# Group 6's maxima one unit later and in another bank, and sixteen idle matmuls in the first four attention units

## The chip, the cores and the metric

The kernel runs on one core of one Trainium2 chip. The metric is the device time of one execution in microseconds (us), and the number compared is the median of several runs. Before the change the median of three runs is 684.25 us (682.8 to 686.36).

## The reference, cut to what matters

The kernel computes one transformer layer on x of shape (4, 1024, 256): cross attention with a context of 64 rows per batch, and a feed-forward part with one shared expert and eight routed ones (two per token). Only the attention is touched by the change:

```
q = (layernorm(x) @ Wq + bq)   in 16 heads of width 16
k = (ctx @ Wk + bk),  v = (ctx @ Wv + bv)      64 keys per batch
a = clip(q k^T / 4, -10000, 10000)
a = softmax(a);  a = 1/64 everywhere if anything in it is not a number
x = x + (a v) @ Wo + bo
x = x + shared(layernorm(x)) + sum over the top 2 experts of w * expert(layernorm(x))
```

The softmax subtracts, for every query row and head, the maximum over the keys. The kernel computes these maxima in a separate, cheaper pass.

## The kernel before, in words

The 4096 rows of x are 32 tiles of 128, in NG = 8 groups of four tiles (n = 0 to 7) and in NU = 16 attention units of two tiles (u = 0 to 15). Every engine has its own instruction stream, written out by hand, and semaphores join them; within an engine the order is that of the code. Most products are made in three half-precision parts (high times high, high times low, low times high).

Before the attention units, TensorE projects the queries of each group and makes the *row scores* `row_scores(js)`: for each tile and each half of the heads one 128x512 matmul, whose maximum over the keys VectorE takes in `row_max` (L1094). There are 64 of them (j = 0 to 63). A group's eight maxima are clipped (`clip_max` on VectorE L1103, or for the last two groups `clip_late` on GpSimd L700), transposed by TensorE in `max_t(n)` (L1581, four transposes) into bank `max_bank(n)`, and copied by VectorE to `m_t` in `copy_max(n)` (L1109). Groups 0 to 4 go before the units, group 5 at the end of unit 0, group 6 at the end of unit 2, group 7 at the end of unit 12. The last row scores are made inside units 0, 1 (four each) and 4 to 11 (one each, in bank 7).

TensorE's `unit(u)` for the attention is: `scores(u)`, 24 matmuls of 32 rows x 256 into banks 0 to 3, which waits until all four exponentials of unit u-1 have been taken; the late row scores; then for r = 0 to 3 `weigh(u-2, r)`, 12 matmuls of 34 or 32 columns with the probabilities of two units back, which waits for GpSimd's low half (`pl_ready`), and `subtract_max(u, r)`, two matmuls of 32 rows x 256, which waits for VectorE's `clip` (L1129) of bank r; the rest of the late row scores; `max_t`; and from unit 4 on `project(u-4)`, one matmul with 512 columns and twelve with 256 into bank 6, which waits for the output's transposes by DMA (`ot_got`, issued on SP at L540 after GpSimd's L722).

ScalarE per unit: four exponentials `exps(u, r)` (L900), three casts to half precision `cast_p` (L907), the high half of the output (L952) and the fourth cast; in units 1 to 3 also a weight cast (L893). GpSimd per unit: in units 0 to 2 two multiplications for the low half of the keys (`keys`, L652), four low halves of the probabilities (L729), the low half of the output (L722), `clip_late(6)` first in unit 2, and the weight split `low_weight(1)` (L707) in unit 3. VectorE per unit: four clips, `copy_max` if there is one, late maxima, residual and statistics of unit u-5 (L1169 on), `normalise(u-2)` (L1141, L1149), and in units 3 and 5 a weight split `split_lo` (L1189). In unit 0 VectorE also makes the scale of the exponentials from a flag that lies in bank 7 (`scale_of_exps`, L1122 to L1124, which raises `scale_ready`), between its first and its second clip.

Bank 7 holds that flag, group 6's and 7's transposed maxima and the row scores from j = 56 on; bank 6 holds the transposed maxima of groups 0 to 5 and from unit 4 on the projection.

Of the kernel before, what the change touches and what calls it, by code (L numbers as in the profile page):

```python
# [12 lines left out]
P = 128  # L13
# [4 lines left out]
def build(nc, x, ctx_t, wq, bq, wk, bk, wv, bv, wo, bo, gate_t, w_all, out):  # L18
# [14 lines left out]
    NG = NT // GT  # L33
# [34 lines left out]
    with ExitStack() as ctx:  # L68
# [6 lines left out]
        bank = [ctx.enter_context(nc.psum_tensor(f"bank{i}", [P, 512], F32)) for i in range(8)]  # L75
# [290 lines left out]

        def max_bank(n):

            return 6 if n < NG - 2 else 7

        def score_bank(j):

# [672 lines left out]
        def _(dve):  # L1045
# [145 lines left out]
            def unit(u):  # L1191
                if u == NU - 1:
                    scale_guess2(slice(0, LN2_FIRST * GT))
                    scale_and_shift2(slice(0, LN2_FIRST * GT))
                for r in range(RT):
                    clip(u, r)
                    if u == 0 and r == 0:
                        scale_of_exps()
                if u == 0:
                    copy_max(NG - 4)  # L1200
                if u == 1:
                    copy_max(NG - 3)
                if u == 3:
                    copy_max(NG - 2)
                if u == 13:
                    copy_max(NG - 1)
                if u < 2:
                    late_max(u)
                if known(u, 5):
                    rows_of(u - 5)  # L1210
                if known(u, 2):
                    normalise(u - 2)
                if u >= 2:
                    late_max(u)
                if u == 3:
                    split_lo(0)
                if u == 5:
                    split_lo(2)
                if NU <= u < NU + 3:
                    low_half(u - NU)  # L1220
# [311 lines left out]
        def _(pe):  # L1532
            def mm(o, a, b, first, last, check=False):
                return pe.matmul(o, a, b, start=first, stop=last, skip_group_check=not check)  # L1534
# [19 lines left out]
            def row_scores(js):  # L1554

                for j in js:
                    t, hf = divmod(j, HF)
                    n, i = divmod(t, GT)
                    if i == 0 and hf == 0:
                        pe.wait_ge(kblk_ready, HF * (n * B // NG + 1))  # L1560
                    pe.wait_ge(qh_ready, HF * n + hf + 1)
                    if t > 0:
                        pe.wait_ge(smax_used, scores_read_for(j))
                    if j == LATE_MAX:
                        pe.wait_ge(mt_copied, NG - 1)
                    mm(bank[score_bank(j)][:, :], qx[:, 0, hf, bass.ts(t, P)],
                       k_blk[:, 0, n * B // NG, hf].rearrange("p h k -> p (h k)"),
                       True, True).then_inc(smax_ready, 1)

            def max_t(n):  # L1570
                if n < NG - 2:
                    pe.wait_ge(mcl_ready, n + 1)
                else:
                    pe.wait_ge(mcl_late, n - NG + 3)
                if n == NG - 2:
                    pe.wait_ge(scale_ready, 1)
                elif 1 <= n < NG - 2:
                    pe.wait_ge(mt_copied, n)
                for i in range(GT):
                    c = 64 * i  # L1580
                    ins = pe.transpose(bank[max_bank(n)][:, c:c + 64].bitcast(F16),  # L1581
                                       m_cl[:, n % 2, i].rearrange("p r h -> p (r h)"), ident[:, :])
                ins.then_inc(mt_ready, 1)
# [116 lines left out]
            def project(u):  # L1700

                pe.wait_ge(ot_got[u % 2], 16 * UT * (u // 2 + 1))
                if u == 0:
                    pe.wait_ge(bo_split, UT)
                    pe.wait_ge(wo_lo, 1)
                    pe.wait_ge(mt_copied, NG - 2)
                if u >= 1:
                    pe.wait_ge(y_added, u)
                mm(bank[6][:, :], ones_h[0:P // 2, :], bo_hl.rearrange("p t c -> p (t c)"), True, False)
                for t in range(UT):  # L1710
                    for i, (a, c) in enumerate(THREE):
                        for hf in range(HF):
                            ins = mm(bank[6][:, bass.ts(t, C)], o_t[:, u % 2, t, c, hf],
                                     wo_hl[:, a, hf], False, i == 2 and hf == HF - 1)
                ins.then_inc(y_ready, 1)
# [8 lines left out]
            def gate(g):  # L1724
# [13 lines left out]
                                     c == 1 and hf == HF - 1)  # L1738
                ins.then_inc(lg_ready, 1)

            def unit(u):
                if known(u, 0):
                    scores(u)
                row_scores(late_scores(u)[:2])
                for r in range(RT):
                    if known(u, 2):
                        weigh(u - 2, r)
                    if known(u, 0):
                        subtract_max(u, r)
                if u < 2:  # L1750
                    row_scores(late_scores(u)[2:])
                if u == 0:
                    max_t(NG - 3)
                if u == 2:
                    max_t(NG - 2)
                if u == 12:
                    max_t(NG - 1)
# [205 lines left out]
```

## Time and profile before

| | |
|---|---|
| median of three runs | 684.25 us |
| the profiled execution's own time | 689.7 us |
| its span, first to last instruction | 688.0 us |
| mean granted clock of TensorE | 0.935 |
| busy: TensorE matmul | 606.8 us (88%) |
| busy: VectorE, ScalarE, GpSimd | 413.8, 346.7, 395.3 us |

The span runs from the first to the last instruction; 1.7 us of the execution's own time lie outside it. The granted clock is given as a share of full speed: 1.00 is 2.4 GHz and 0.50 is 1.2 GHz. The page cuts the span into 40 slices of 17.2 us; the attention units are the slices 5 to 11 (from about 78 to 205 us). In those slices the page's clock row reads 9, 5, 5, 9, 9, 7, 7. A matmul's busy time is counted as long as it is in the pipeline, so an engine that reads as fully busy need not be at its peak.

### The profile page before, as it was taken

Reading aid. Unit: us, or ns where it says so; the run is one execution under the profiler, and the core shown is the slowest. Engines: PE = TensorE matmul, PEld = TensorE weight load, DVE = VectorE, ACT = ScalarE, POOL = GpSimd, SP = SyncE. Lnnn points to the kernel's source line nnn. Section 1 sums busy time; section 2 is a strip of 40 time slices with the busy share of each in tenths; the row PEclk is TensorE's granted clock in tenths of the full one; section 3 lists DMA queues with packets and bytes.
Section 4 is the critical chain, followed back from the end, with each engine's and each line's share of the span. In section 5 each row is a group of like instructions: output and inputs, shape, how many; then the busy total and the mean of one; then the engine's idle time right before and its main releaser. Section 6 shows DMA issues by size and latency. Waiting matters only on the chain.

```text
span 688.0 us, 15439 instructions
## 1 busy us (share of the span) xinstructions
PE 606.8 (88%) x5212; PEld 412.9 (60%) x5212; DVE 413.8 (60%) x916; ACT 346.7 (50%) x572; POOL 395.3 (57%) x333
## 2 busy tenths in 40 slices
PE   3698679999897897997998999999999999999990
PEld 1244235665564554554754788777788787776870
DVE  5998866986875453899654344544444545443450
ACT  3987577886697662653254343333332433333330
POOL 6589598989660121434063546666656666657543
PEclk9899855997789998999999999999999999999996
DMA  8344401251129796885149544766755657657533
GB/s 266 90 70 84 131 2 40 51 129 33 32 61 216 172 206 204 214 161 116 46 102 175 103 78 88 109 91 100 101 95 96 97 96 101 93 95 101 87 40 39
DMA packets 121102, 72.44 MB, mean 105 GB/s; under 512 B 91779, under 2 KB 114246, under 8 KB 121030
## 3 DMA queue, kind: packets, MB, share of 16 engines
q1 hardware_dynamic: 101974, 44.01, 29.2%
q0 software_dynamic: 19056, 27.43, 24.8%
q8 instruction: 49, 0.80, 0.5%
q14 instruction: 23, 0.19, 0.1%
HBM read 29.47 MB, written 22.15 MB: 75 GB/s over the span
## 4 chain that ended last, share of the span: by engine, by line
PE 49%; POOL 13%; DVE 11%; issue 7%; ACT 6%; SPq 6%; DMA 5%; another core or an unknown queue 2%; POOLq 0%; DVEq 0%; ACTq 0%
PE bank L1534 47%; POOL arena L729 6%; SPq L549 4%; DMA out<-w_stage,map_i 2%; DMA arena<-arena 2%; POOL arena L722 2%; POOL arena L638 2%; POOL arena L652 1%; ACT arena L823 1%; DVE hidden L1428 1%; PE bank L1896 1%; DVE arena L1189 1%; DVE bank L1129 1%; POOL qx L645 1%
## 5 line engine op out<-in xcount | busy, mean ns | idle before, releaser
L1534 PE MATMUL bank<-qx,arena 128*128 128x256 f16 (+1 forms) x1584 | 158.8, 291 | 3.5 <-issue 1.6
L1534 PE MATMUL bank<-arena 128*128 128x34 f16 (+6 forms) x1282 | 137.1, 250 | 27.1 <-DVE bank L1129 7.3
L753 POOL DMA_INDIRECT out<-w_stage,map_i x71 | 113.7, 1601 | 68.2 <-DMA out<-w_stage,map_i 28.2
L1534 PEld LDWEIGHTS bank<-qx,arena 128*128 (+1 forms) x1584 | 126.4, 102 | 26.6 <-issue 11.2
L740 POOL DMA_INDIRECT qx<-rows_d,map_i x71 | 74.1, 1043 | 85.2 <-DVE lane_w L1495 42.9
L1534 PEld LDWEIGHTS bank<-arena 128*128 128x128 f16 (+2 forms) x1282 | 76.6, 106 | 76.5 <-issue 39.3
L1503 DVE TENSOR_TENSOR hidden<-bank,hidden 128x512 f32<-128x512 f32 x71 | 49.1, 691 | 113.1 <-ACT hidden L1026 91.3
L1026 ACT ACTIVATE hidden<-bank 128x512 f32<-128x512 f32 x71 | 42.4, 597 | 129.6 <-PE bank L1534 90.2
L1534 PE MATMUL bank<-arena,w_stage 128*128 x852 | 104.9, 273 | 3.0 <-ACT w_stage L1032 2.7
L1534 PE MATMUL bank<-qx,w_sh 128*128 128x512 f16 x384 | 91.4, 385 | 9.7 <-DVE hidden L1428 7.4
L1534 PEld LDWEIGHTS bank<-arena,w_stage 128*128 128x128 f16 x852 | 81.8, 98 | 20.7 <-issue 6.9
L1534 PE MATMUL bank<-arena,qx 128*128 (+1 forms) x316 | 83.0, 387 | 4.8 <-issue 3.3
L729 POOL TENSOR_TENSOR arena<-hidden,arena 128x512 f16<-128x512 f32 x64 | 74.4, 1185 | 17.1 <-ACT arena L907 17.0
L707 POOL TENSOR_TENSOR arena<-w_stage,arena 128x1024 f16<-128x1024 f32 x12 | 27.4, 2281 | 90.2 <-ACT arena L893 90.2
L1522 DVE TENSOR_TENSOR w_stage<-hidden,w_stage 128x512 f16<-128x512 f32 x71 | 49.4, 696 | 44.5 <-ACT w_stage L1038 29.3
L1534 PEld LDWEIGHTS bank<-qx,w_sh 128*128 128x128 f16 x384 | 37.1, 99 | 52.6 <-DVE hidden L1428 12.7
L1038 ACT CAST w_stage<-hidden 128x512 f16<-128x512 f32 x71 | 43.9, 619 | 40.5 <-DVE hidden L1503 34.4
L900 ACT ACTIVATE hidden<-bank,arena 128x512 f32<-128x512 f32 x64 | 43.5, 687 | 29.7 <-PE bank L1534 25.3
L1534 PEld LDWEIGHTS bank<-arena,qx 128*128 128x128 f16 x316 | 30.9, 98 | 44.1 <-issue 14.6
L1129 DVE TENSOR_SCALAR bank<-bank 128x512 f32<-128x512 f32 x64 | 40.0, 692 | 18.3 <-PE bank L1534 17.8
L1534 PE MATMUL bank<-w_sh,hidden 128*128 128x256 f16 x384 | 49.5, 282 | 1.3 <-DVE hidden L1428 0.7
L1434 DVE TENSOR_TENSOR bank<-bank,hidden 128x512 f32<-128x512 f32 x32 | 22.3, 695 | 46.1 <-ACT hidden L984 43.7
(194 smaller groups left out, 713.6 us busy)
## 6 DMA issues: line engine op xcount, KB each, us to landing
w_stage<-in_w_all SPq DMA_DIRECT2D x27, 512.0 KB, 4.7
out<-x_sb POOLq DMA_DIRECT2D x16, 512.0 KB, 7.9
x_sb<-in_x SPq DMA_DIRECT2D x8, 512.0 KB, 7.3
rows_d<-arena SPq DMA_DIRECT2D x8, 512.0 KB, 4.0
qx<-rows_d,map_i POOLq DMA_INDIRECT x71
qx<-qx SPq DMA_TRANSPOSE x71
out<-w_stage,map_i POOLq DMA_INDIRECT x71, 3.9
arena<-arena SPq DMA_TRANSPOSE x56, 2.5
```

The costliest lines, as they stand in the source:

```text
L549: sp.dma_start_transpose(qx[:, :, :, bass.ts(GT * g + t, P)].rearrange("p s h t -> p (s h) t"), x2_hl[g % XB][:, t].rearrange("p a c -> p ...
L707: pool.tensor_tensor(w[:, 1], w_stage[:, q % 4, :], w[:, 0], ALU.subtract).then_inc(w_lo[q % 4], 1)
L729: pool.tensor_tensor(p_l[:, u % PB, r], p_f[:, k % FB], p_h[:, u % PB, r], ALU.subtract).then_inc(pl_ready, 1)
L740: pool.indirect_dma_start(out=gathered(r), out_offset=None, in_=rows_d, in_offset=bass.IndirectOffsetOnAxis(ap=map_i[:, 0, i:i + 1], axis= ...
L753: pool.indirect_dma_start(out=out, out_offset=bass.IndirectOffsetOnAxis(ap=map_i[:, 1, i:i + 1], axis=0), in_=y_sb[:, r], in_offset=None, ...
L900: act.activation(p_f[:, k % FB], bank[r][:, :], ACT.Exp, scale=exp_scale).then_inc(exp_ready, 1)
L1026: act.activation(act_g[:, k % 2], bank[k % 2][:, :], ACT.Silu).then_inc(sp_silu, 1)
L1038: act.copy(h_sp[:, k % 3, 0], h_f[:, k % 2]).then_inc(sp_hh, 1)
L1129: dve.tensor_scalar(bank[r][:, :], bank[r][:, :], CLIP, -CLIP, ALU.min, ALU.max).then_inc(st_clipped, 1)
L1503: dve.tensor_tensor(h_f[:, k % 2], bank[2 + k % 2][:, :], act_g[:, k % 2], ALU.mult).then_inc(sp_h, 1)
L1522: dve.tensor_tensor(h_sp[:, k % 3, 1], h_f[:, k % 2], h_sp[:, k % 3, 0], ALU.subtract).then_inc(sp_hl, 1)
L1534: return pe.matmul(o, a, b, start=first, stop=last, skip_group_check=not check)
```

## The change: the diff

Group 6's maxima are transposed at the end of TensorE's unit 3 instead of unit 2, into bank 6 instead of bank 7, and VectorE copies them in its unit 4 instead of 3. `project(0)`, the first user of bank 6 after that, waits for the copy. The wait for `scale_ready` (the flag in bank 7 has been read) moves to the first idle matmul, and stands again before row score 56. A new function `keep_busy(u, times)` issues matmuls with 128 rows and 512 columns into bank 7 whose result nobody reads; it is called with 2 after r = 1 and after r = 3 in each of the units 0 to 3, sixteen matmuls in all.

```diff
         def max_bank(n):
-            return 6 if n < NG - 2 else 7
+            return 6 if n < NG - 1 else 7
...
-                if u == 3:
+                if u == 4:
                     copy_max(NG - 2)
...
                     if j == LATE_MAX:
-                        pe.wait_ge(mt_copied, NG - 1)
+                        pe.wait_ge(scale_ready, 1)
...
-                if n == NG - 2:
-                    pe.wait_ge(scale_ready, 1)
-                elif 1 <= n < NG - 2:
+                if 1 <= n < NG - 1:
                     pe.wait_ge(mt_copied, n)
...
                     pe.wait_ge(wo_lo, 1)
-                    pe.wait_ge(mt_copied, NG - 2)
+                    pe.wait_ge(mt_copied, NG - 1)
...
+            def keep_busy(u, times):
+
+                if u < 4:
+                    if u == 0:
+                        pe.wait_ge(scale_ready, 1)
+                    for _ in range(times):
+                        mm(bank[7][:, :], qx[:, 0, 0, 0:P], k_blk[:, 0, 0, 0].rearrange("p h k -> p (h k)"), True, True)
+
             def unit(u):
...
                     if known(u, 0):
                         subtract_max(u, r)
+                    if r % 2:
+                        keep_busy(u, 2)
...
-                if u == 2:
+                if u == 3:
                     max_t(NG - 2)
```

## Rows read from the trace of the kernel before

**Rows 1.** Chain of waits, 80 to 270 us: start, us, what (time order).
```profile
84.96 4.49 POOL arena L729 x4
...
117.93 1.12 POOL arena L729
119.05 2.37 issue
...
256.28 5.82 DMA qx<-arena
```

**Rows 2.** GpSimd's timeline in units 0 to 10: start, us, instruction, idle before.
```profile
84.96 4.49 POOL L729 TENSOR_TENSOR arena<-hidden,arena 128x512 f16<-128x512 f32 x4 [1.93 <-ACT arena L907]
...
97.85 1.08 POOL L700 TENSOR_SCALAR arena<-arena 128x256 f16<-128x256 f32 x1
...
113.45 3.38 POOL L729 TENSOR_TENSOR arena<-hidden,arena 128x512 f16<-128x512 f32 x3 [0.27 <-ACT arena L907]
...
121.45 4.37 POOL L729 TENSOR_TENSOR arena<-hidden,arena 128x512 f16<-128x512 f32 x3 [2.40 <-ACT arena L907]
...
128.29 3.39 POOL L729 TENSOR_TENSOR arena<-hidden,arena 128x512 f16<-128x512 f32 x3 [0.23 <-ACT arena L907]
...
134.19 3.38 POOL L729 TENSOR_TENSOR arena<-hidden,arena 128x512 f16<-128x512 f32 x3 [0.28 <-ACT arena L907]
...
153.49 3.39 POOL L729 TENSOR_TENSOR arena<-hidden,arena 128x512 f16<-128x512 f32 x3 [1.88 <-ACT arena L907]
```

**Rows 3.** ScalarE's timeline: same columns.
```profile
82.50 1.88 ACT L900 ACTIVATE hidden<-bank,arena 128x512 f32<-128x512 f32 x3 [0.65 <-PE bank L1534]
...
105.45 0.69 ACT L900 ACTIVATE hidden<-bank,arena 128x512 f32<-128x512 f32 x1 [0.30 <-PE bank L1534]
...
118.03 2.84 ACT L900 ACTIVATE hidden<-bank,arena 128x512 f32<-128x512 f32 x4 [2.59 <-PE bank L1534]
```

**Rows 4.** TensorE's timeline, matmuls only: same columns.
```profile
81.88 1.77 PE L1534 MATMUL bank<-arena 32*128 32x256 f16 x6 [1.53 <-DVE bank L1129]
84.00 1.18 PE L1534 MATMUL bank<-arena,qx 128*128 128x512 f16 x2 [0.34 <-DVE arena L1094]
...
98.99 0.61 PE L1581 MATMUL bank<-ident,arena 128*128 128x128 f16 x4 [1.41 <-POOL arena L700]
...
106.28 1.47 PE L1534 MATMUL bank<-qx,arena 32*128 32x256 f16 x24 [0.87 <-ACT hidden L900]
...
112.61 2.74 PE L1534 MATMUL bank<-arena 128*128 128x256 f16 x12
115.28 1.47 PE L1534 MATMUL bank<-qx,arena 32*128 32x256 f16 x24
...
120.40 1.48 PE L1534 MATMUL bank<-arena 128*128 128x256 f16 x12
```

**Rows 5.** Stretches: length, busy us per engine (instructions), granted clock, DMA share, GB/s.
```profile
78.20:85.50 7.30, 5.06 (x40) 1.86 (x40) 6.70 (x13) 3.69 (x7) 5.22 (x6) 0.63 0.00 0
85.50:91.70 6.20, 4.63 (x37) 1.58 (x36) 4.90 (x9) 4.35 (x9) 6.20 (x7) 0.78 0.00 0
91.70:99.50 7.80, 5.97 (x85) 3.27 (x84) 4.42 (x10) 6.01 (x11) 7.80 (x8) 0.50 0.01 2
...
106.30:115.30 9.00, 9.00 (x98) 4.92 (x101) 5.60 (x10) 8.40 (x15) 8.61 (x8) 0.50 0.19 38
115.30:121.80 6.50, 6.50 (x95) 4.02 (x94) 4.92 (x13) 3.82 (x8) 4.09 (x5) 0.82 0.20 40
...
128.60:134.50 5.90, 5.70 (x96) 3.80 (x94) 5.69 (x15) 5.33 (x10) 5.62 (x6) 1.00 0.24 49
...
165.00:205.00 40.00, 36.46 (x460) 22.93 (x457) 29.88 (x89) 30.82 (x53) 27.51 (x25) 0.74 0.20 41
```

**Rows 6.** VectorE's timeline, the clips of unit 5: start, us, instruction, idle.
```profile
116.78 2.49 DVE L1129 TENSOR_SCALAR bank<-bank 128x512 f32<-128x512 f32 x4 [3.38 <-PE bank L1534]
```

**Rows 7.** DMA issues, 100 to 200 us: line, engine, operation, count, us to landing.
```profile
arena<-arena SPq DMA_TRANSPOSE x29, 2.5
```

## The prediction

> **What bounds the kernel now.** I read the page's clock row first (0.5 in the slices of the first attention units), then the chain of waits, then one timeline per engine. From 84.96 to 119.05 us the chain lies on GpSimd: it begins with the four low halves of unit 0 and ends with one of unit 4, and only then does something else take over, 2.37 us of waiting [rows 1]. GpSimd's own timeline shows how little it waits there: 0.27 us before unit 4's low halves and then 2.40 us before unit 5's, both for a cast on ScalarE [rows 2]. That cast was late because ScalarE had waited 2.59 us for TensorE [rows 3], and TensorE had not been idle at all: from 106.3 to 115.3 it is busy 9.00 of 9.00 us, at a granted clock of 0.50, its lower level of 1.2 GHz [rows 5]. Inside that stretch the first projection's twelve matmuls take 2.74 us; the same twelve take 1.48 us in the next unit, once the clock is up [rows 4]. So in units 0 to 3 GpSimd is the bound and TensorE has room; in unit 4 a slow TensorE uses up the room and costs 2.4 us.
>
> From unit 6 on the clock is 1.00 [rows 5] and the cycle is 5.90 us (128.29 to 134.19), of which GpSimd works all but 0.28 [rows 2]. TensorE is the tighter one there, by those 0.28 us: its scores, the four clips on VectorE (2.49 us [rows 6]) and the projection follow each other.
>
> **The change, part by part.**
>
> *The idle matmuls, their own price.* There is no row of two such matmuls back to back. The twelve 256-column matmuls give 2.74/12 = 0.228 us per 256 columns at the low clock and 1.48/12 = 0.123 at the high one [rows 4], so a pair of 512 columns is 4 x 0.228 = 0.91 us low and 0.49 high; a unit's four cost 1.8 or 1.0. Over four units that is 7.3 or 3.9 us of TensorE. The matmuls of one engine are executed in order, so `subtract_max(u, 2)` stands behind the first pair, and the exponential of r = 2 waits for it. The second pair is followed by row scores, which wait for VectorE, or by the next unit's scores, which wait for the last exponential.
>
> *Unit 0.* Here the pair is on the path. The second `subtract_max` starts at 81.88 [rows 4], at the low clock, and the three exponentials after it run from 82.50 in one piece, 0.62 us apart [rows 3]; the one of r = 2 starts at 83.12. With the pair between, I place the end of that `subtract_max` at 81.88 + 0.43 + 0.91 + 0.43 + some 0.12 until ScalarE sees it = 83.77: 0.65 us late. The cast and GpSimd's first low half (84.96, after 1.93 us idle [rows 2]) move with it: +0.65, on the bound engine. Ends: 0, if the pair fits in the gap before VectorE's next clip, and 0.91, a whole pair. The wait for `scale_ready` costs nothing: the second clip, for which TensorE waits anyway, comes after that instruction on VectorE.
>
> *Units 1 to 3: does the clock rise?* In unit 0 the mean is 0.63, in unit 1 it is 0.78, in unit 2 it is 0.50 and it stays there until unit 5's 0.82 [rows 5]. Units 1 and 2 keep TensorE busy only 4.63 of 6.20 and 5.97 of 7.80 us, the second at the low level and with 34-column matmuls; the clock came back after the projection, the first dense wide work. In the changed kernel each of the four units has 2048 wide columns more in a tight burst. I take the clock to be up from about unit 1 through unit 3: a unit's TensorE chain is then about 4.9 us from the start of its scores to the end of its last exponential (as in unit 7) plus 0.5 for the pair, far under GpSimd's 8 us or so in units 2 and 3, and the pairs cost nothing there. The two ends are the clock staying low (a rival below) and the clock staying high through unit 4 too.
>
> *Group 6's maxima.* In unit 2 the four transposes wait 1.41 us for GpSimd's `clip_late` [rows 4], which ran at 97.85 [rows 2], and take 0.54. `scores(3)` stands behind them. They leave unit 2 (up to 1.95 us, less what `scores(3)` would then wait for the last exponential: I take 1.2) and stand in unit 3, where `clip_late` is long done, 0.54 us before scores that wait for an exponential anyway. Between 0 and -1.95 us for TensorE; for the end nothing by itself, since GpSimd is the bound there. `copy_max(6)`, 0.4 us on VectorE, moves from unit 3 to unit 4, where VectorE is busy 5.60 of 9.00 us [rows 5]; the projection waits for it, but a `subtract_max` that waits for the last clip and the fourth `weigh` stand between, so 0; if the copy came last it would cost its 0.4. Nothing on SP or the GpSimd queue is moved.
>
> *Unit 4 and 5.* With the clock up, `scores(4)` start some 3 us before 106.28 [rows 4]. The first projection needs the transposed output of unit 0, which GpSimd finishes at about 104.1 (103.4 + 0.65); SP's two issues and a landing of 2.5 us [rows 7] put it at 107.6. Even at the low clock (3.2 us with its 512-column start) `scores(5)` then begin at 110.8, and at the high one at 109.4, against 115.28 [rows 4]. So unit 5's cast is there when GpSimd wants it, and both waits go: GpSimd reaches unit 5 at 121.45 + 0.65 - 0.27 - 2.40 = 119.4, a gain of 2.0 us.
>
> *After that.* TensorE is now ahead of GpSimd by about 2 us, so for some units GpSimd runs at its own 5.62 us instead of 5.90, and the next stalls from a slow TensorE (0.23 before unit 6, 0.28 in each of units 7 to 9, 1.88 before unit 10 [rows 2]) are met with a reserve. All of it together is 0.23 + 3 x 0.28 + 1.88 = 2.95: the gain lies between 2.0 and 5.0. I take the middle, 3.5 us. What is late next is TensorE's own chain, and in units 12 to 15 the clock (0.74 from 165 to 205 us [rows 5]), which the change doesn't touch.
>
> *Carried to the end.* From the end of the attention the chain goes on over transposes of the second layernorm by DMA, whose last lands after 256.28 [rows 1], then routing and the experts; all of it starts from the last attention units and nothing in it runs by a clock of its own, so I carry the gain whole. The profiled execution took 689.7 us, 5.4 over the median; 689.7 - 3.5 = 686.2, and for the median 684.25 - 3.5 = 680.8.
>
> **A rule that speaks against it.** From 106.3 to 115.3 TensorE had no gap and ran at 0.50 all the same [rows 5], until after the projection. The Trainium skill, TensorE: Matmul & The Clock Gate, section "Why this matters for your kernels", ties the drop to gaps without matmuls. The idle matmuls stand in a queue that is executed in order, right behind a `subtract_max`, and so they fill no gap in which TensorE waits for GpSimd. By that rule the clock would be as before and the sum the one of the second rival; the trace agrees only in part, since a stretch without gaps stayed slow.
>
> **Rivals.**
>
> *Nothing that can be measured.* The clock comes up for part of units 1 to 3 only, or unit 4 falls back while the projection waits for its transposes. Then unit 0's +0.65 and part of the pairs eat most of the 2.0 us, and the reserve isn't there for the later stalls: -1 to 0, about 683.8. For it: the clock at 1.2 GHz for 27 us although TensorE read as nearly full.
>
> *Slower: the clock stays low and TensorE becomes the bound.* Place: the loop from scores over the second pair to the last exponential. Delay of `scores(2)`: about 1.0 (0.9 in unit 0 less the 0.34 idle in it [rows 4], and 0.9 in unit 1, partly beside VectorE's row maxima). Unit 2: +0.91, less the transposes that go, leaves `scores(3)` +0.8. Unit 3: +0.91 for the first pair, then the second pair and 0.54 of transposes outlast the last exponential (105.45 + 0.69 [rows 3]) by 0.6: `scores(4)` +2.3, and everything behind it: 684.25 + 2.3 = 686.5. It decides as soon as TensorE's unit at the low clock with its pairs (about 7.6 us) plus the inherited delay is longer than GpSimd's unit. Against it: unit 1 had 0.78 even without idle matmuls.
>
> *More than forecast.* The reserve survives to unit 12, and all 2.95 us of later waits go, and a slow spell of the last units with them (one costs 1 to 2 us): -5.0 - 1.5 = -6.5, 677.8.
>
> **How the numbers follow.** Forecast case 0.52 (own range 679.0 to 682.5), nothing 0.24, slower 0.14, more 0.10. A measurement of this kernel tells about 0.5% from no change, 3.4 us: faster means under 680.8. That takes half the forecast case and more (0.33) and the fourth (0.10): 0.43. Slower by 3.4 us needs the low clock and another bad spell: 0.07. The rest, 0.50, is the same. The range leaves one in five out: from 677.0 (beyond the fourth case) to 686.3.
>
> **What would show it.** The granted clock from 91 to 106 us at or near 1.00 instead of 0.50; ScalarE's wait of 2.59 us and GpSimd's of 2.40 us before unit 5 gone; GpSimd's first low half some 0.65 us later; no wait of TensorE for `clip_late` in unit 2; `scores(5)` beginning 4 to 6 us earlier against the start of unit 0. Wrong would be a clock still at 0.50 in units 2 and 3 with `scores(4)` later than before; or the waits gone and the gain given back in units 12 to 15.

## The result, and the profile after

The changed kernel takes 694.06 us (median of 4 runs, 693.59 to 694.46) against 684.91 us of the kernel before (4 runs, 682.8 to 686.36): a ratio of 1.0115, with the 95% interval [1.0081, 1.0148]. It is 9.1 us slower by the medians, where the forecast said 3.5 us faster. Medians and ranges here are of all runs, while the ratios leave out runs over 1.5% above the fastest of the same kernel and are not plain quotients of the medians (which would be 1.0134 here). The profiled run took 693.59 us, with a span of 691.8.

The change's direct effects are there, most of them as forecast. First the stretches of the changed kernel (units 0, 1, 2 and 3, then unit 4 with the wait before it, then 176 to 216 us); the columns are those of [rows 5]:

```profile
79.80:87.10 7.30, 5.37 (x40) 1.78 (x41) 5.92 (x12) 2.87 (x5) 4.68 (x5) 0.72 0.00 0
87.70:93.70 6.00, 5.55 (x42) 1.80 (x40) 5.05 (x9) 4.25 (x9) 6.00 (x6) 0.82 0.02 3
93.70:99.20 5.50, 4.80 (x85) 2.74 (x84) 4.37 (x10) 5.17 (x10) 5.50 (x6) 1.00 0.00 0
99.20:105.40 6.20, 5.70 (x88) 3.34 (x88) 4.30 (x10) 6.20 (x12) 6.20 (x7) 0.85 0.01 3
105.40:123.20 17.80, 8.86 (x99) 4.78 (x102) 14.78 (x11) 8.26 (x15) 11.11 (x10) 0.60 0.15 31
176.00:216.00 40.00, 33.98 (x445) 21.67 (x446) 28.10 (x82) 28.93 (x49) 27.14 (x24) 0.80 0.21 40
```

The granted clock is 1.00 in unit 2, where it was 0.50 [rows 5]. The fifth stretch is the odd one: 17.80 us with TensorE busy for half of it and VectorE for 14.78. ScalarE's timeline (columns as in [rows 3]) has one wait that the kernel before doesn't have:

```profile
85.60 1.26 ACT L900 ACTIVATE hidden<-bank,arena 128x512 f32<-128x512 f32 x2 [0.81 <-PE bank L1534]
...
117.11 0.69 ACT L900 ACTIVATE hidden<-bank,arena 128x512 f32<-128x512 f32 x1 [8.65 <-PE bank L1534]
```

It waits for TensorE, and TensorE's timeline says for whom that one waits (compare [rows 4]):

```profile
104.85 0.63 PE L1579 MATMUL bank<-ident,arena 128*128 128x128 f16 x4
105.42 1.47 PE L1534 MATMUL bank<-qx,arena 32*128 32x256 f16 x24
...
116.49 3.54 PE L1534 MATMUL bank<-arena 32*128 32x256 f16 x44 [8.94 <-DVE bank L1129]
...
123.17 1.23 PE L1534 MATMUL bank<-qx,arena 32*128 32x256 f16 x24
```

So VectorE's clip of unit 4 came 8.94 us late. VectorE's timeline shows no wait at all in front of that clip; it shows one instruction of 11.06 us, the weight split of unit 3 (`split_lo`):

```profile
104.01 0.76 DVE L1149 TENSOR_TENSOR arena<-bank,arena 128x256 f32<-128x256 f32 x2
104.68 11.06 DVE L1189 TENSOR_TENSOR w_sh<-w_stage,w_sh 128x1024 f16<-128x1024 f32 x1
115.66 2.48 DVE L1129 TENSOR_SCALAR bank<-bank 128x512 f32<-128x512 f32 x4
```

In the kernel before, the same instruction on VectorE takes 1.70 us:

```profile
105.99 1.70 DVE L1189 TENSOR_TENSOR w_sh<-w_stage,w_sh 128x1024 f16<-128x1024 f32 x1
```

It has the same operands and the same size. What differs is GpSimd beside it. The changed kernel's GpSimd timeline, to be held against [rows 2]:

```profile
87.45 4.49 POOL L729 TENSOR_TENSOR arena<-hidden,arena 128x512 f16<-128x512 f32 x4 [2.81 <-ACT arena L907]
...
104.76 1.15 POOL L722 TENSOR_TENSOR arena<-arena 128x512 f16<-128x512 f32 x1
105.87 1.14 POOL L729 TENSOR_TENSOR arena<-hidden,arena 128x512 f16<-128x512 f32 x1
106.99 2.12 POOL L707 TENSOR_TENSOR w_sh<-w_stage,w_sh 128x1024 f16<-128x1024 f32 x1
109.07 3.36 POOL L729 TENSOR_TENSOR arena<-hidden,arena 128x512 f16<-128x512 f32 x3
112.40 1.14 POOL L722 TENSOR_TENSOR arena<-arena 128x512 f16<-128x512 f32 x1
113.51 1.14 POOL L729 TENSOR_TENSOR arena<-hidden,arena 128x512 f16<-128x512 f32 x1
121.34 3.38 POOL L729 TENSOR_TENSOR arena<-hidden,arena 128x512 f16<-128x512 f32 x3 [6.69 <-ACT arena L907]
...
129.11 4.37 POOL L729 TENSOR_TENSOR arena<-hidden,arena 128x512 f16<-128x512 f32 x3 [2.17 <-ACT arena L907]
```

From 87.45 to 114.65 us GpSimd works without a gap; in the profile each instruction begins a little before the last one ends. The split ends at 104.68 + 11.06 = 115.74, which is 1.09 us after GpSimd's last instruction: about the time the split itself needs. And in the kernel before:

```profile
104.48 2.12 POOL L707 TENSOR_TENSOR w_sh<-w_stage,w_sh 128x1024 f16<-128x1024 f32 x1
106.72 1.99 POOL L729 TENSOR_TENSOR arena<-hidden,arena 128x512 f16<-128x512 f32 x1
```

The first of these ends at 106.60, the next starts at 106.72. At those 0.12 us, in which GpSimd waited for a cast that a slow TensorE had made late, the split got in; it ended at 107.69, again 1.09 us after GpSimd's instruction, and GpSimd's next one took 1.99 us instead of 1.15.

The loss then goes around: split, clips, scores, exponentials, cast, GpSimd, which waits 6.69 us before unit 4 (0.27 before [rows 2]). The chain of the changed kernel has it as the piece behind GpSimd's last low half:

```profile
113.54 1.11 POOL arena L729
114.65 6.65 issue
```

From the first scores to the start of GpSimd's last L722, which I take as the attention's length, it is 134.3 us in the profile of after and 124.8 before, 9.5 more; the sum of GpSimd's waits in that stretch is 30.8 against 20.3 us. Of the 10.5, 6.4 lie before unit 4 and 0.9 before unit 0; 3.5 are spread over units 6 to 15 (and 0.2 are gained before unit 5). The two profiled executions themselves differ by 3.9 us only (693.59 and 689.7), because the part behind the attention is 7 us shorter in the profile of after. So that the 9.1 us between the medians are this loss isn't read from the two profiles; it rests on the experiments.

### The profile page after: what moved, and what is told of

It is laid out like the page before. It is cut to its first block, busy times and chain, and to the rows that moved or that the text cites. A ratio compares the mean times of both kernels' runs of the same rounds, so it can differ in the third digit from the quotient of the medians.

```text
span 691.8 us, 15471 instructions
## 1 busy us (share of the span) xinstructions
PE 603.3 (87%) x5228; PEld 412.5 (60%) x5228; DVE 424.1 (61%) x916; ACT 347.0 (50%) x572; POOL 393.4 (57%) x333
## 4 chain that ended last, share of the span: by engine, by line
PE 52%; POOL 13%; DVE 10%; issue 8%; DMA 8%; ACT 5%; SPq 3%; POOLq 0%; DVEq 0%; ACTq 0%
PE bank L1534 50%; POOL arena L729 6%; DMA out<-w_stage,map_i 3%; DMA arena<-arena 2%; DMA qx<-qx 2%; POOL arena L722 2%; POOL arena L638 2%; SPq L549 1%; POOL arena L652 1%; PE bank L1904 1%; ACT arena L823 1%; DVE hidden L1428 1%; DVE arena L1189 1%; DVE bank L1129 1%; POOL qx L645 1%
## 5 line engine op out<-in xcount | busy, mean ns | idle before, releaser
L1534 PE MATMUL bank<-qx,arena 128*128 128x256 f16 (+1 forms) x1584 | 155.2, 281 | 1.6 <-DVE arena L1094 1.0
L1534 PE MATMUL bank<-arena,qx 128*128 (+1 forms) x332 | 88.9, 391 | 3.5 <-issue 2.2
L729 POOL TENSOR_TENSOR arena<-hidden,arena 128x512 f16<-128x512 f32 x64 | 73.5, 1171 | 27.5 <-ACT arena L907 27.5
L707 POOL TENSOR_TENSOR arena<-w_stage,arena 128x1024 f16<-128x1024 f32 x12 | 27.4, 2282 | 89.4 <-ACT arena L893 89.4
L1129 DVE TENSOR_SCALAR bank<-bank 128x512 f32<-128x512 f32 x64 | 40.0, 691 | 18.4 <-PE bank L1534 18.0
```

The costliest lines, as they stand in the source:

```text
L707: pool.tensor_tensor(w[:, 1], w_stage[:, q % 4, :], w[:, 0], ALU.subtract).then_inc(w_lo[q % 4], 1)
L729: pool.tensor_tensor(p_l[:, u % PB, r], p_f[:, k % FB], p_h[:, u % PB, r], ALU.subtract).then_inc(pl_ready, 1)
L1129: dve.tensor_scalar(bank[r][:, :], bank[r][:, :], CLIP, -CLIP, ALU.min, ALU.max).then_inc(st_clipped, 1)
```

## The experiments

Theory A: the split is shut out by GpSimd's instructions as long as these follow each other without a gap, and the waits that the change closed were the gap that it used. Rivals: B, the idle matmuls cost it themselves (TensorE's time, bank 7); C, the move of the maxima does it in some other way (bank 6, the copy in unit 4). The kernel before measures from 684.9 to 691.7 us from one chip and set of runs to the next, so each ratio is against the kernel before beside it, on the same chip. Where a profile is quoted, it is that of one execution.

**e1_gap and e13_gap_again: an opening made on purpose.** The changed kernel; GpSimd, before its weight split of unit 3, waits until VectorE's split is done.

```diff
+                    pool.wait_ge(w_lo[0], 1)
                     low_weight(1)
```

> The changed kernel, with one wait more: GpSimd waits in unit 3, before low_weight(1), until VectorE's weight split split_lo(0) is done. Theory A (the split is held out while GpSimd's instructions follow each other without a gap, 11.06 us instead of 1.70, and everything behind it on VectorE with it): the split takes 1.2 to 1.7 us and ends before low_weight(1) begins; GpSimd loses about 1.5 us there, its 6.69 us wait before unit 4 falls under 1 us, the time is 5 to 8 us under the changed kernel's 694.1, so about 687, and perhaps under the kernel before. Rival B (the idle matmuls and the clock made it slower): the time stays within 2 us of 694.

> e1 once more, with more rounds: the changed kernel with GpSimd's wait for the split. Theory A: on this chip too, within 2 us of the kernel before and 3 to 7 us under the changed kernel; rival B: over the kernel before by 5 to 9 us.

The first gave 688.92 us (679.01 to 690.45, 4 runs, no interval) beside 687.41 of the kernel before, the second 685.83 (12 runs) beside 687.37, a ratio of 0.9971 [0.9945, 0.9998]. VectorE's and, in the second fence, GpSimd's timeline of e1_gap (its lines stand one further down):

```profile
104.09 3.43 DVE L1190 TENSOR_TENSOR w_sh<-w_stage,w_sh 128x1024 f16<-128x1024 f32 x1
```

```profile
107.61 2.13 POOL L707 TENSOR_TENSOR w_sh<-w_stage,w_sh 128x1024 f16<-128x1024 f32 x1 [1.16 <-DVE w_sh L1190]
```

The split was still held out, until the gap came, and ended in it (104.09 + 3.43 = 107.52; e13 the same, 3.73 us), so it took longer than the 1.2 to 1.7 us expected. But the waits of GpSimd before units 4 and 5 are gone in both profiles, and the attention takes 126.1 us in e13's instead of 134.3. For 1.16 us of waiting on GpSimd the loss is gone, with the idle matmuls and the moved maxima both in place. That is against B and C.

**e2_max_only: the move alone.** The changed kernel without the calls of `keep_busy`.

```diff
-                    if r % 2:
-                        keep_busy(u, 2)
```

> The changed kernel without its idle matmuls: only group 6's maxima are moved. Theory A: scores(3) come some 1.2 us earlier than before, so ScalarE's cast of unit 3 is there when GpSimd has done low_weight(1), its gap of 0.1 us at 106.6 closes, and the split is held out as in the changed kernel: about 692 to 695. If a gap remains: 684 to 685, no difference from before. Rival B (idle matmuls): 684 to 685 with the split at 1.7 us.

689.84 us (10 runs) beside 687.41, ratio 1.0045 [1.0003, 1.0088]; 692 to 695 had been expected. VectorE's and GpSimd's timeline:

```profile
104.56 8.54 DVE L1189 TENSOR_TENSOR w_sh<-w_stage,w_sh 128x1024 f16<-128x1024 f32 x1
```

```profile
118.70 3.38 POOL L729 TENSOR_TENSOR arena<-hidden,arena 128x512 f16<-128x512 f32 x3 [6.69 <-ACT arena L907]
```

Here the clock stayed at 0.50 from unit 1 on, and there is not one idle matmul; yet the split was held out, to 1.09 us after the end of GpSimd's run at 112.01. Taking the transposes out of unit 2 is enough to close the gap. B alone is out. The attention takes 132.0 us in this profile, 7.2 more than before, of which only some 2.4 us come out between the medians.

**e3_idle_only: the idle matmuls alone**, in units 0 to 2 of the kernel before.

```diff
+                    if r % 2:
+                        keep_busy(u, 2)
```

> The kernel before with the idle matmuls in units 0 to 2 and group 6's maxima left where they were. Theory A: the clock rises as in the changed kernel, ScalarE's casts come early and GpSimd has no gap: the split is held out for some 8 to 10 us, 691 to 695. Rival B: the idle matmuls cost their own time only, up to 0.65 us on the path in unit 0: 684 to 686, split at 1.7 us.

Four runs, 685.64, 692.56, 695.55 and 994.91 us, ratio 1.0103 [1.0028, 1.0177]. Its profile (685.64 us) has the split at 1.68 us, in a gap of 0.13. So the expectation that it is held out was wrong in that execution, which is the fastest of the four; the clock had fallen back to 0.50 from about 100 us, and the transposes in unit 2 kept their wait. I count it as inconclusive.

**e4_split_early, e7_split_unit1 and e5_split_unit2: the split at another place**, in unit 2 and in unit 1 of the kernel before, and in unit 2 of the changed one (`split_lo(2)` in unit 5 stays).

```diff
-                if u == 3:
+                if u == 2:
                     split_lo(0)
```

(For e7 the line reads `if u == 1:`.)

> The kernel before with split_lo(0) on VectorE in unit 2 instead of unit 3; no idle matmul, nothing else. Theory A: it starts at about 98.5 us, in the middle of GpSimd's unbroken run from 84.96 on, and ends only when GpSimd has its first gap (about 106.7 or later): 8 us or more for one instruction, unit 3's clips behind it, and the time rises by 4 to 9 us. Rival B: the split takes 1.7 us wherever it stands and the time is that of before, 684 to 686.

> The kernel before with split_lo(0) at the end of VectorE's unit 1; nothing else. It can start when its high half is there, at about 93.8, in the middle of GpSimd's low halves (to 95.9) and key products (to 97.9), all with two inputs; clip_late(6), with one, runs at 97.85. Theory A: the split ends at 97.9 + 1.1 = 99.0 and reads as some 5.2 us; the clips of unit 2, before at 93.20, come after it, everything on TensorE and ScalarE 5 to 6 us later, GpSimd idle as long, and the time 4 to 6 us over the kernel before. Rival (it is held out only by the low halves of unit 3, or takes 1.2 us wherever it stands): 1.2 to 1.7 us and no difference in time.

> The changed kernel with split_lo(0) on VectorE in unit 2, where GpSimd runs clip_late(6), an instruction with one input tensor. Theory A, refined (only GpSimd's instructions with two input tensors hold the split out): it starts at about 99, waits for the end of the key product at 100.4 and takes 2.2 us in all; unit 3's clips are 1.4 us later, which TensorE's lead covers; GpSimd's wait of 6.69 us before unit 4 goes, and the time is 5 to 9 us under the changed kernel's. Rival: the idle matmuls are what costs, and the time stays within 2 us of the changed kernel's.

e4: 688.65 us, 1.0001 [0.9966, 1.0036]; e7: 695.23, 1.0030 [0.9994, 1.0065]; e5: 695.38, 1.0028 [0.9994, 1.0063] (10, 12 and 12 runs, one of e5's at 785.91). Theory A, read strictly, failed in all three: the split took 1.22, 2.07 and 1.32 us in the middle of a run without gaps. In e7 and e5 it got in between two instructions of GpSimd, and GpSimd's next one took about 1 us longer. In e4 it didn't wait at all. VectorE's and GpSimd's timeline of e4:

```profile
98.25 1.22 DVE L1189 TENSOR_TENSOR w_sh<-w_stage,w_sh 128x1024 f16<-128x1024 f32 x1
```

```profile
97.96 1.08 POOL L700 TENSOR_SCALAR arena<-arena 128x256 f16<-128x256 f32 x1
```

The split ran beside GpSimd's one-input clip until 99.04 us, the clip took its usual 1.08 us [rows 2] and the split its 1.22, as long as it takes where GpSimd stands still (1.21 in e6 below). So not every instruction of GpSimd holds it up. e5's VectorE timeline, with both splits:

```profile
99.54 1.32 DVE L1189 TENSOR_TENSOR w_sh<-w_stage,w_sh 128x1024 f16<-128x1024 f32 x1
...
122.17 6.10 DVE L1189 TENSOR_TENSOR w_sh<-w_stage,w_sh 128x1024 f16<-128x1024 f32 x1
```

The first got in at the next boundary; the second was held out, and GpSimd then waited 6.69 us before unit 6, so the 5 to 9 us expected of e5 did not come: it is 1.1 us under the changed kernel of its set (696.49, a8 below), which by its number alone fits its rival, the idle matmuls. In the other profiles the second split got in. So a run without gaps can shut the split out and need not.

**a8_changed_again and a17_changed_third: the changed kernel, repeated in two later sets.**

> The changed kernel once more, so that the others of this set have it on the same chip: 9 us over the kernel before, as in its first timing, and the split of 11 us in VectorE's unit 3 in the profile. If it is under 4 us here, part of the first difference was the chip.

> The changed kernel on the same chip as e16: 5 to 9 us over the kernel before, split of 11 us.

696.49 us (12 runs) beside 691.69, 1.0065 [1.0036, 1.0095], and 696.90 (6 runs) beside 690.93, 1.0105 [1.0072, 1.0138]: 4.8 and 6.0 us over the kernel before, against 9.1 in the first timing and the 9 expected of a8. The loss is there each time, its size is not settled. The split takes 11.05 and 11.32 us, and ends 1.09 us after GpSimd's run both times.

**e6_max_and_gap: e2 with e1's opening** (both edits are shown above).

> Group 6's maxima moved, no idle matmuls, and GpSimd waits for the split in unit 3. Theory A: split at 1.2 to 1.7 us instead of 8.54, GpSimd loses about 1.2 us and then runs on; TensorE at the low clock reaches scores(5) as in the kernel before: within 2 us of the kernel before, 3 to 5 us under the changed kernel's maxima alone. Rival (moving the maxima costs by itself): over the kernel before by as much as e2 was, 2 to 3 us.

689.81 us (12 runs), 0.9974 [0.9938, 1.0010]; the split took 1.21 us. The move of the maxima without the hold-out costs nothing that these runs can tell.

**e9_clip_on_dve and e16_clip_dve_again: group 6's clip on VectorE.** The changed kernel; the clip leaves GpSimd's unit 2 (`clip_late`) for VectorE's.

```diff
-                    if r == 0 and u in (2, 12):
-                        clip_late(NG - 2 if u == 2 else NG - 1)
+                    if r == 0 and u == 12:
+                        clip_late(NG - 1)
...
+                if u == 2:
+                    dve.wait_ge(smax_used, HF * GT * (NG - 1))
+                    dve.wait_ge(mt_ready, NG - 3)
+                    dve.tensor_scalar(m_cl[:, 0, :, :, 0:HD], m_raw[:, 0].unsqueeze(2).to_broadcast([P, GT, RT, HD]),
+                                      -CLIP, CLIP, ALU.max, ALU.min).then_inc(mcl_late, 1)
```

> The changed kernel with group 6's maxima clipped on VectorE in unit 2 instead of on GpSimd (clip_late(6) goes; group 7's stays). In the traces so far the split was held out only in GpSimd's run since that clip, where its instructions hand over to each other with an overlap of 0.031 to 0.033 us; at overlaps of 0.039 us and more it got in at the first boundary, also without any gap. Theory A1 (any unbroken run of GpSimd holds it out): split still some 10 us, time as the changed kernel. Theory A2 (it is the run since the one-input clip): overlaps stay at 0.04 to 0.06, the split gets in at the first boundary and takes 1.2 to 2.2 us, GpSimd's 6.69 us wait goes, and the time is 5 to 8 us under the changed kernel's (9.1 and 4.8 us over the kernel before on two chips), near or a little under the kernel before.

> e9 once more: 3 to 6 us under the kernel before (0.9934 on the chip of its first timing), and 8 us or more under the changed kernel.

684.34 us (681.46 to 686.05, 6 runs) beside 687.37, 0.9934 [0.9910, 0.9958], and in the next set 683.50 (6 runs) beside 690.93, 0.9908 [0.9875, 0.9941]. This beats both kernels; a17, beside e16 on the same chip, is 13.4 us slower. VectorE's and GpSimd's timeline of e9:

```profile
96.79 0.47 DVE L1202 TENSOR_SCALAR arena<-arena 128x256 f16<-128x256 f32 x1
...
104.51 1.31 DVE L1189 TENSOR_TENSOR w_sh<-w_stage,w_sh 128x1024 f16<-128x1024 f32 x1
```

```profile
104.70 2.13 POOL L729 TENSOR_TENSOR arena<-hidden,arena 128x512 f16<-128x512 f32 x1
...
118.91 5.48 POOL L729 TENSOR_TENSOR arena<-hidden,arena 128x512 f16<-128x512 f32 x4
...
139.53 3.39 POOL L729 TENSOR_TENSOR arena<-hidden,arena 128x512 f16<-128x512 f32 x3 [1.75 <-ACT arena L907]
```

GpSimd works without a wait from 87.28 to 139.53 - 1.75 = 137.78 us; the split got in at the first boundary, and the L729 that started then took 2.13 us instead of 1.15. This is the course of GpSimd's waits that I had forecast for the change itself.

**e12_max_clip_dve: e9 without the idle matmuls** (e2's edit on e9).

> As e9, without the idle matmuls: group 6's maxima moved, their clip on VectorE. A2: the split takes 1.2 to 2.2 us; the clock stays at 0.50 in units 2 to 4 and TensorE reaches scores(5) late, so GpSimd waits some 2 us before unit 5 as in the kernel before; time within 2 us of the kernel before. If the idle matmuls are worth what was forecast for them, e9 is 2 to 4 us under this one.

689.09 us (12 runs), 1.0008 [0.9978, 1.0037], beside e9's 684.34 on the same chip. The split was let in at the first boundary it met, but took 2.78 us. Between these two kernels the sixteen idle matmuls are worth 4.8 us, of which the profiles show 1.8 in the attention (126.3 against 124.5). The other pair that differs by them alone, e13 with 0.9971 and e6 with 0.9974, each on its own chip, shows no such difference. So what the idle matmuls are worth stays open.

**e10, e14, e15: which instruction of GpSimd does the shutting out?** A2: the run stays shut once a one-input instruction (the clip) has passed in it. A3: it is the key multiplications with the clip right behind them. e10 moves the key multiplications from GpSimd's unit 2 to unit 3 of the changed kernel; e14 puts a one-input clip back into e9's GpSimd stream, at its old place, its result unused; e15 a two-input subtraction instead.

```diff
-                    if u < B - 1:
-                        keys(1, u + 1)
+                    if u in (0, 1, 3):
+                        keys(1, min(u + 1, 3))
```

```diff
+                    if r == 0 and u == 2:
+                        pool.wait_ge(smax_used, HF * GT * (NG - 1))
+                        m6 = m_raw[:, 0].unsqueeze(2).to_broadcast([P, GT, RT, HD])
+                        pool.tensor_scalar(spare[:, :, :, 0:HD], m6, -CLIP, CLIP, ALU.max, ALU.min)
```

> The changed kernel with the last batch's two key products (L652) in GpSimd's unit 3 instead of unit 2, before low_weight(1); clip_late(6) now follows the low halves of unit 1 directly. Theory A1 and A2 alike, if the clip or the unbroken run is what counts: the split is held out, until GpSimd's first wait, 10 us or more. If it is the key products with the clip right behind them (A3): the split gets in, 1.2 to 2.2 us, and the time falls by 5 to 8 us.

> e9 with one instruction more on GpSimd: where clip_late(6) stood in unit 2, a clip of the same maxima with one input tensor, into memory that nobody reads until much later. A2 (the one-input instruction in the run is what shuts the split out): the split is held out again until GpSimd's first wait, some 10 us, GpSimd waits some 6.7 us before unit 4, and the time goes back up by 3 to 9 us over e9. A4 (what changed in e9 was the timing on VectorE and TensorE): the split gets in at the first boundary and the time is e9's within 2 us.

> e9 with one instruction more on GpSimd at the same place, a subtraction of the same shape with two input tensors, into memory that nobody reads until much later. A2: the split gets in at the first boundary, 1.2 to 2.2 us, the time that of e9 plus about 1 us. If any further instruction there shuts it out: some 10 us for the split and 3 to 9 us over e9.

e10: 687.12 us, 0.9988 [0.9958, 1.0018], split 1.70 us. It got in at a boundary without a gap (102.24 us); but the move had made a gap of 0.32 us right behind the clip, at 96.30, so the run that the split met had no clip in it, and e10 doesn't tell A2 from A3. e14: 688.13, 0.9934 [0.9898, 0.9971], split 1.42 us. e15: 690.03, 0.9995 [0.9967, 1.0023], split 2.13 us (12 runs each). e14's GpSimd stream has the changed kernel's instructions in their order, and still let the split in at the first boundary: A2 fell, and so did A3.

The times are less clear than the profiles. e14 is 4.6 us over e16 of the same set by the medians, its runs spread from 680.5 to 699.0 us, and the quotient of the medians of all runs is 0.996. e15 is 6.5 us over e16, where 1 was expected, though its split got in and its attention is no longer in the profile (125.4 against 125.2 us). Where e15's time goes isn't shown.

**e17_extra_clip_u2 and e18_extra_clip_u3: GpSimd's stream untouched.** The changed kernel with one more clip on VectorE, into memory that nobody reads until much later; in unit 2, or directly before the split in unit 3. A5 (recorded before the run): VectorE's own clip in unit 2 is what lets the split in; A7: GpSimd's clip in unit 2 shuts it out.

```diff
+                if u == 2:
+                    dve.wait_ge(smax_used, HF * GT * (NG - 1))
+                    dve.tensor_scalar(spare[:, :, :, 0:HD], m_raw[:, 0].unsqueeze(2).to_broadcast([P, GT, RT, HD]),
+                                      -CLIP, CLIP, ALU.max, ALU.min)
```

> The changed kernel with one instruction more on VectorE: in unit 2, after the clips of the scores, the same clip of group 6's maxima as in e9, into memory that nobody reads until much later; GpSimd's clip_late(6) stays. A5 (VectorE's own clip in unit 2 is what lets the split in later): the split takes 1.2 to 2.2 us, no wait of 6.69 us on GpSimd, 8 us or more under the changed kernel. A7 (GpSimd's clip_late(6) with its wait and its semaphore is what shuts it out): split of some 10 us and the changed kernel's time, 5 to 9 us over the kernel before.

> The changed kernel with that same additional clip directly before split_lo(0) in unit 3. If every instruction of VectorE with operands in SBUF alone is held out, the clip (0.6 us where it ran so far) is the one that takes some 10 us and the split follows it in 1.2 us; if only two-input ones are, the clip takes 0.6 us and the split some 10. Time: the changed kernel's in both cases. If the extra instruction shifts or frees the handover, both are short and the time is 8 us or more under the changed kernel.

e17: 691.42 us (683.84 to 697.52, 12 runs) beside 690.78, 0.9980 [0.9941, 1.0019]; the changed kernel was not run beside it, so the 8 us expected of A5 can't be compared on one chip. e18: 697.83 (6 runs), 1.0101 [1.0059, 1.0144]. The VectorE timelines, e17's first:

```profile
93.52 0.29 DVE L1202 TENSOR_SCALAR logits<-arena 128x256 f16<-128x256 f32 x1
...
103.15 1.39 DVE L1190 TENSOR_TENSOR w_sh<-w_stage,w_sh 128x1024 f16<-128x1024 f32 x1
```

```profile
104.26 10.14 DVE L1218 TENSOR_SCALAR logits<-arena 128x256 f16<-128x256 f32 x1
114.31 1.21 DVE L1190 TENSOR_TENSOR w_sh<-w_stage,w_sh 128x1024 f16<-128x1024 f32 x1
```

With one clip more on VectorE and all of GpSimd's instructions as in the changed kernel, the split got in (e17). And where it isn't let in, it is not the split as such: in e18 a one-input clip of 0.29 us stands in front and is the one that is held out, for 10.14 us, while the split behind it takes 1.21. In both kernels the VectorE instructions that read or write a bank (L1129 and L1149 of the kernel before) ran beside the rest of GpSimd's run at their usual 0.4 to 0.7 us.

**What stays open.** What decides whether a waiting VectorE instruction gets in at a boundary of GpSimd's run. It was held out in after, a8, a17, e2, e18, at e5's second split, and in e1 and e13 until the made gap; it got in, without a gap, at e5's first split and in e4, e7, e9, e10, e12, e14, e15, e16 and e17. Which boundary it met first is part of it, perhaps: in the six profiles after, a8, a17, e1, e13 and e18 the instruction held out began 0.08 to 0.37 us before an L722 of GpSimd, and in e9, e14, e15, e16 and e17 the split began one boundary later, 0.19 to 1.0 us before the L729 behind that L722. It isn't the whole of it, since in e2 (held out) and e12 (let in) the split met the same boundary, that between L707 and L729. How closely GpSimd's instructions follow each other is no sure sign: in most of the run they overlap by 0.031 to 0.034 us wherever the split was shut out, but also in e14 and e17. e17's runs spread over 13.7 us and e14's over 18.5; that the split is held out in some of them and not in others is only argued, since one execution was profiled.

Against the kernel before, the kernels in whose profile the split of unit 3, or the clip ahead of it, was held out for the rest of the run measure 1.0045 to 1.0115 (after, a8, a17, e2, e18), and those in which it got in or had an opening 0.9908 to 1.0030 (e5, whose second split was held out, 1.0028), with e3's four runs (1.0103) as the exception. That the hold-out makes the changed kernel slow is therefore shown, and why it happens at one boundary and not at another is not.

## Why the prediction was wrong, step by step

*Unit 0.* Right in kind. GpSimd's first low half starts 87.45 - 79.81 = 7.64 us after the first scores, against 84.96 - 78.21 = 6.75 before: +0.89. I took 0.65, the bound was 0.91.

*Units 1 to 3, the clock.* Right. 0.82, 1.00 and 0.85 against 0.78 and 0.50 [rows 5], and the pairs cost GpSimd nothing: it runs through units 1 to 3 without a wait. The stretches rose after TensorE had been given wide idle matmuls in the gaps of units 0 and 1; without them (e2) the clock stayed at 0.50. The part "A rule that speaks against it" would have had the clock as before, since the idle matmuls stand behind others in a queue; the trace does not agree with that.

*Group 6's maxima.* Right. TensorE's transposes of unit 3 start at 104.85 with no wait for `clip_late`, and scores(4) start 105.42 - 79.81 = 25.6 us after the first scores, against 28.1 before: 2.5 us earlier, where I had some 3. The copy in unit 4 shows no cost: e6 and e9 have it too and are not slower than the kernel before.

*Unit 4 and 5: this step failed.* "So unit 5's cast is there when GpSimd wants it, and both waits go". scores(5) start 123.17 - 79.81 = 43.4 us after the first scores, against 37.1 before: 6.3 later instead of 4 to 6 earlier. The step counted TensorE, ScalarE and GpSimd; of VectorE the prediction had only the 5.60 busy us of 9.00 [rows 5], taken as room for the copy, and it put the time of VectorE's weight split at nothing new. It left out that this split can be kept out as long as GpSimd's run goes on, and that closing GpSimd's waits can take its chance away. The split was held for 11.06 - 1.70 = 9.4 us more, and 6.4 us of that came out as a wait on the bound engine. e1 and e13 show it by giving the opening back (1.0115 in after, 0.9971 in e13), e9 and e16 by another way (0.9934 and 0.9908).

The Trainium skill, SBUF — State Buffer, section "Summary: rules for kernel authors", says that when GpSimd reads SBUF beside a VectorE instruction with two SBUF inputs, the second to issue "fully blocks" until the first finishes. The trace agrees that the split and GpSimd's two-input instructions exclude each other, and GpSimd's L729 of 1.99 us shows it the other way round. It differs in the length, since the split stood back for eight further instructions of GpSimd, not for the one that was running, and in e4, where the split ran beside GpSimd's one-input clip. By that rule alone the split would have waited for one instruction, some 1 us, as it did in e9, and GpSimd's 6.69 us would not have come.

*After that: the reserve.* Not tested by the changed kernel, but by e9, where both waits did go. GpSimd's waits from unit 6 to unit 15 are 18.3 us there and 15.7 before: 2.6 us come back, most of it as waits of 1.75, 1.99 and 1.75 before units 8, 10 and 11, where there were 0.29, 1.88 and 0.28, and 4.40 instead of 3.44 before unit 13. In the profile, e9's attention takes 124.5 us, 0.3 less than before. I had carried the reserve forward as a gain; these waits take it back. Where e9's measured 3 to 7 us come from isn't seen in these single profiles, and stays open; that they lie near my 3.5 doesn't bear out the sum.

*Carried to the end.* Not shown. I had carried the gain whole, since nothing behind the attention "runs by a clock of its own". But the part behind the attention varies between 478 and 488 us over all the profiles, and e2's attention is 7.2 us longer in its profile with 2.4 us between the medians.

*The rivals.* The slower one that I had put down needed a low clock and TensorE as the bound. The clock was high in units 1 to 3, and TensorE stood idle for 8.94 us in unit 4: the rival had the right sign by the wrong mechanism, and at 686.5 us it was 7.6 too low. A forecast that names which engine is late next has to ask that of the engine that looks half idle too.

## What to carry to other kernels

A wait on the bound engine may be what lets another engine work: where VectorE instructions that touch only SBUF stand beside a GpSimd stream that is about to become gapless, list them, ask what is queued behind each, and price each at both ends, one boundary and the rest of GpSimd's run. A group whose duration grows from 1.7 to 11 us at the same shape is a wait that the profile counts as busy time; compare durations by instruction, not only the idle columns. The cure that does not hang on luck is one deliberate wait of GpSimd at a place of your choice (1.16 us in e1, 1.17 in e13). Taking one instruction off GpSimd's stream (e9) let the split in as well and measured better, but putting one back did not shut it out again (e14, e15). Measure, since which boundary lets the other engine in could not be foretold here.

## What the runs showed of the hardware

- A VectorE instruction that reads and writes only SBUF can be kept out by GpSimd over a whole run of back-to-back instructions: 11.06, 11.05, 11.32, 8.54 and 10.14 us for instructions of 1.2 and 0.3 us. The split always ends 1.09 us after the last instruction of that run.
- At gaps of 0.12 (before) and 0.13 us (e3) in GpSimd's stream it got in, and no profile has it held out past a gap. GpSimd's next instruction takes about 1 us more where the split gets in just ahead of it (1.99 or 2.13 instead of 1.15).
- Sometimes it gets in with no gap at all (e9: 104.51, 1.31 us). Counted from the first scores, the split began 0.6 us later than in the changed kernel in e17, and at the same time in e9.
- A one-input clip of VectorE with half-precision output can be held out as well as a two-input subtraction (10.14 us in e18; 0.29 in e17). A one-input clip of GpSimd did not hold the split up (e4: 1.22 us beside L700).
- TensorE at 2.4 GHz in 93.7 to 99.2 us, with wide idle matmuls before it and in it, where the same unit ran at 1.2 GHz without them.
